# A bias add moved to GpSimd, a scale folded into a mask, and one rounding pass on VectorE

## The reference

```python
fake_quant(x): scale = absmax(x, axis) / bound;  q = round(clip(x / scale));  return q * scale
xq = fake_quant(conv, bits=8, axis=-1)      # one scale a row (sample, channel)
kq = fake_quant(kernel, bits=8, axis=0)     # one scale an output column
y  = xq @ kq + fake_quant(bias, bits=16)
out = x + fake_quant(y, bits=8, axis=-1)    # one scale a row
```

## Time and profile before

| what | value |
|---|---|
| median of 3 runs | 280.97 us (279.19 to 281.17) |
| the profiled execution | 278.56 us |
| its span | 276.7 us |
| TensorE busy | 251.1 us, 91% |
| VectorE busy | 238.8 us, 86% |
| ScalarE busy | 185.2 us, 67% |
| GpSimd busy | 153.8 us, 56% |

### The profile page before, as it was taken

The page is one execution under the profiler, slowest core; times in us unless marked ns, Lnnn a source line. Parts: engine busy times, 40 slices in busy tenths (PEclk is TensorE's granted clock), DMA queues, the critical chain, the costliest instruction groups (busy, mean ns, idle before and its releaser), DMA issues.

```text
span 276.7 us, 4240 instructions
## 1 busy us (share of the span) xinstructions
PE 251.1 (91%) x1372; PEld 163.5 (59%) x1372; DVE 238.8 (86%) x509; ACT 185.2 (67%) x278; POOL 153.8 (56%) x71
## 2 busy tenths in 40 slices
PE   7866769999999999999999999999999999997540
PEld 3555557666666666666666666666666666663210
DVE  1799964799999999999999999999999989999984
ACT  6257586477777777777777777777777767564762
POOL 2533333356666666666666666666666666533453
PEclk9979999999999999999999999999999999999996
DMA  6997322406666565566666766666666663333355
GB/s 253 416 408 301 123 84 103 153 0 227 223 203 212 211 202 212 203 217 217 209 204 210 230 228 228 228 227 226 219 203 197 218 218 117 144 142 139 107 220 219
DMA packets 15799, 56.04 MB, mean 203 GB/s; under 512 B 1954, under 2 KB 1954, under 8 KB 15778
## 3 DMA queue, kind: packets, MB, share of 16 engines
q1 hardware_dynamic: 15488, 55.71, 56.8%
q10 hardware_dynamic: 290, 0.07, 0.1%
HBM read 38.99 MB, written 16.78 MB: 202 GB/s over the span
## 4 chain that ended last, share of the span: by engine, by line
PE 81%; DVE 8%; ACT 4%; DMA 3%; issue 2%; SPq 0%; DVEq 0%
PE dense_ps L427 36%; PE conv_ps L396 31%; PE turn_ps L416 5%; PE conv_ps L386 5%; DMA k_raw<-ffn_kernel 3%; DVE dense_ps L550 2%; DVE y L559 2%; DVE y_max L604 2%; ACT kq L279 2%; PE small_ps L407 2%; PE dense_ps L449 1%; DVE k_max L523 1%; ACT a_int L304 1%; PE dense_ps L440 1%; ACT x_hi L265 1%
## 5 line engine op out<-in xcount | busy, mean ns | idle before, releaser
L427 PE MATMUL dense_ps<-kq,a_t 128*128 128x512 bf16 x512 | 120.6, 379 | 6.1 <-DVE y L559 5.0
L218 POOL TENSOR_TENSOR x_lo<-xwin,x_hi 128x1032 fp32r<-128x1032 f32 x32 | 76.6, 2393 | 80.8 <-ACT x_hi L265 80.8
L227 POOL TENSOR_TENSOR o_sb<-y,o_sb 128x1024 f32<-128x1024 f32 x31 | 73.9, 2384 | 32.8 <-ACT y L315 32.7
L427 PEld LDWEIGHTS dense_ps<-kq,a_t 128*128 128x128 bf16 x512 | 48.9, 101 | 53.7 <-issue 6.7
L295 ACT CAST a_t<-turn_ps 128x1024 bf16<-128x1024 int16 x32 | 32.4, 1012 | 48.5 <-PE turn_ps L416 48.5
L564 DVE TENSOR_REDUCE small_ps<-conv_ps 128x8 f32<-128x1024 f32 x32 | 39.4, 1232 | 13.8 <-PE conv_ps L396 13.5
L550 DVE SCALAR_TENSOR_TENSOR dense_ps<-dense_ps,row_scale,k_scale_b 128x512 f32<-128x512 f32 x64 | 47.7, 745 | 3.6 <-PE dense_ps L427 3.6
L312 ACT ACTIVATE y_int<-y,y_inv 128x1024 int16<-128x1024 f32 x31 | 35.6, 1148 | 22.3 <-DVE y_inv L611 22.1
L559 DVE TENSOR_TENSOR y<-dense_ps,bq 128x512 f32<-128x512 f32 x64 | 43.9, 685 | 2.8 <-ACT bq L288 1.6
L604 DVE TENSOR_REDUCE y_max<-y 128x1 f32<-128x1024 f32 x32 | 38.7, 1210 | 0.7 <-issue 0.2
L304 ACT ACTIVATE a_int<-conv_ps,inv 128x128 int16<-128x128 f32 x128 | 36.0, 363 | 1.1 <-DVE inv L590 1.1
(11 more groups left out here) (55 smaller groups left out, 160.2 us busy)
## 6 DMA issues: line engine op xcount, KB each, us to landing
xwin<-x_windows SPq DMA_DIRECT2D x32, 516.0 KB, 4.8
o_sb<-x_rows SPq DMA_DIRECT2D x32, 512.0 KB, 5.3
out<-o_sb SPq DMA_DIRECT2D x31, 512.0 KB, 2.9
k_raw<-ffn_kernel SPq DMA_DIRECT2D x4, 1024.0 KB, 10.5
w_raw<-taps SPq DMA_DIRECT2D x2, 256.0 KB, 3.2
b_row<-ffn_bias SPq DMA_DIRECT2D x1, 512.0 KB, 15.9
out<-o_sb SPq DMA_DIRECT2D x2, 256.0 KB, 2.7
condt<-cond_t ACTq DMA_DIRECT2D x1, 32.0 KB
```

The source lines that it names most:

```text
L218: pool.tensor_tensor(x_lo[:, at].rearrange("p n b -> p (n b)"), xwin[:, t % XWIN, :], x_hi[:, at].bitcast(F32).rearrange("p n b -> p (n b) ...
L227: pool.tensor_tensor(o_sb[:, at, :], y[:, t % YRING, :], o_sb[:, at, :], ALU.add).then_inc(s["o_made"], 1)
L427: mm = pe.matmul(dense_ps[:, h, :], a_t[:, t % LEVELS, q].rearrange("b j o -> b (j o)"), kq[:, q, half(h)], start=(q == 0), stop=(q == Q - 1))
```

## The change

The bias of the second half is added by GpSimd, in SBUF, in place. VectorE's scaling of that half now writes `y` in SBUF, since GpSimd's add reads it there. For the last tile both stay on VectorE, as before. GpSimd's new `add_bias(t, 1)` is the first step of its iteration t + 5, in front of `split` and `add_x`. `TAIL` becomes 6, so `out_scale`, `quantise`, `add_x` and the store of each tile come one iteration later. TensorE's `dense(t, 1)` waits for the scaling of the tile before, no longer for its bias. The factor 1/127 and the lower limit of the scale move from their own instruction (L582, removed) to the mask and the masking instruction, which becomes a `scalar_tensor_tensor`. VectorE rounds the levels of all eight samples in one instruction of 128x1024, and ScalarE's `round_levels` is gone.

```diff
-TAIL = LAG[1] + 1
+TAIL = LAG[1] + 2
...
+        def pool_adds(t, h):
+            return h == 1 and t < LAST
...
+            def add_bias(t, h):
+                wait(pool, f"scaled{h}", t + 1)
+                wait(pool, "b_made", 1)
+                pool.tensor_tensor(y[:, t % YRING, half(h)], y[:, t % YRING, half(h)],
+                                   bq[:, half(h)], ALU.add).then_inc(s[f"biased{h}"], 1)
...
             for k in range(TILES + TAIL):
+                if there(k - LAG[1] - 1) and pool_adds(k - LAG[1] - 1, 1):
+                    add_bias(k - LAG[1] - 1, 1)
                 if there(k + 2):
                     split(k + 2)
...
-            def round_levels(t):
-                ...
-                for n in range(NS // 2, NS):
-                    ins = act.activation(a_int[:, at, n * BLOCKS:(n + 1) * BLOCKS],
-                                         conv_cols(at)[:, n, :], ACT.Copy,
-                                         scale=inv8[:, at, n:n + 1])
...
             def dense(t, h):
                 wait(pe, "a_made", t + 1)
-                wait(pe, f"biased{h}", t)
+                wait(pe, "scaled1" if h else "biased0", t)
...
+            dve.wait_ge(s["mask_made"], 1)
+            dve.tensor_scalar(mask_q[:], mask[:], 1.0 / 127, None, ALU.mult
+                              ).then_inc(s["mask_q_made"], 1)
...
             def scale_half(t, h):
                 wait(dve, f"dense_made{h}", t + 1)
-                dve.scalar_tensor_tensor(out=dense_ps[:, h, :], in0=dense_ps[:, h, :],
+                if pool_adds(t, h):
+                    wait(dve, "o_made", t - YRING + 1)
+                    to = y[:, t % YRING, half(h)]
+                else:
+                    to = dense_ps[:, h, :]
+                dve.scalar_tensor_tensor(out=to, in0=dense_ps[:, h, :],
...
-                dve.tensor_tensor(col_max[:, t % 2], cmax_ps..., mask[:]..., ALU.mult)
+                dve.scalar_tensor_tensor(out=col_max[:, t % 2], in0=cmax_ps...,
+                                         scalar=127 * TINY, in1=mask_q[:]...,
+                                         op0=ALU.max, op1=ALU.mult)
...
-                dve.tensor_scalar(scale8[:, at], rmax_ps, 1.0 / 127, TINY, ALU.mult,
-                                  ALU.max).then_inc(s["scale_made"], 1)
+                dve.reciprocal(inv8[:, at], rmax_ps).then_inc(s["inv_made"], 1)
...
-                half_n = NS // 2
-                dve.tensor_tensor(a_int[:, at, 0:HALF]..., conv_cols(at)[:, 0:half_n, :], ...)
+                dve.tensor_tensor(a_int[:, at, :]..., conv_cols(at), ...)
...
                     scale_half(k - LAG[1], 1)
-                    add_bias(k - LAG[1], 1)
+                    if not pool_adds(k - LAG[1], 1):
+                        add_bias(k - LAG[1], 1)
```

More of the change, by code:

```diff
@@ L54, in build @@
         mask = sb("mask", [P, NS], F32)
+        mask_q = sb("mask_q", [P, NS], F32)
         same = sb("same", [P, CG], F32)
@@ L356, in _ @@
                     quantise(k - TAIL)
-                if there(k):
-                    round_levels(k)
             quantise_last()
@@ L380, in conv @@
                 x_at = t % XSPLIT
-                wait(pe, "a_rounded_dve", t - 1)
                 wait(pe, "a_rounded", t - 1)
@@ L559, in add_bias @@
                 dve.tensor_tensor(y[:, t % YRING, half(h)], dense_ps[:, h, :], bq[:, half(h)],
-                                  ALU.add).then_inc(s[f"biased{h}"], 1)
+                                  ALU.add).then_inc(s["biased_last" if h else "biased0"], 1)
             def column_max(t):
@@ L570, in column_max @@
                 if t == 0:
[L571 to L574, removed]
+                    dve.wait_ge(s["mask_q_made"], 1)
+                dve.scalar_tensor_tensor(out=col_max[:, t % 2],
+                                         in0=cmax_ps.unsqueeze(2).to_broadcast([P, NS, Q]),
+                                         scalar=127 * TINY,
+                                         in1=mask_q[:].unsqueeze(1).to_broadcast([P, NS, Q]),
+                                         op0=ALU.max, op1=ALU.mult
+                                         ).then_inc(s["col_max_masked"], 1)
             def levels(t):
@@ L581, in levels @@
                 wait(dve, "row_max_made", t + 1)
-                dve.tensor_scalar(scale8[:, at], rmax_ps, 1.0 / 127, TINY, ALU.mult,
-                                  ALU.max).then_inc(s["scale_made"], 1)
+                dve.reciprocal(inv8[:, at], rmax_ps).then_inc(s["inv_made"], 1)
                 wait(dve, "scaled1", t - RSRING + 1)
                 dve.tensor_tensor_reduce(out=picked[:, at], in0=rmax_ps, in1=mask[:],
-                                         scale=1.0 / 127, scalar=0.0, op0=ALU.mult, op1=ALU.add,
+                                         scale=1.0, scalar=0.0, op0=ALU.mult, op1=ALU.add,
                                          accum_out=row_scale[:, r_at:r_at + 1]
                                          ).then_inc(s["picked_made"], 1)
-                wait(dve, "scale_made", t + 1)
-                dve.reciprocal(inv8[:, at], scale8[:, at]).then_inc(s["inv_made"], 1)
                 wait(dve, "inv_made", t + 1)
                 wait(dve, "a_turned", t - 1)
-                half_n = NS // 2
-                dve.tensor_tensor(a_int[:, at, 0:HALF].rearrange("p (n b) -> p n b", b=BLOCKS),
-                                  conv_cols(at)[:, 0:half_n, :],
-                                  inv8[:, at, 0:half_n].unsqueeze(2)
-                                  .to_broadcast([P, half_n, BLOCKS]), ALU.mult
-                                  ).then_inc(s["a_rounded_dve"], 1)
+                dve.tensor_tensor(a_int[:, at, :].rearrange("p (n b) -> p n b", b=BLOCKS),
+                                  conv_cols(at),
+                                  inv8[:, at].unsqueeze(2).to_broadcast([P, NS, BLOCKS]),
+                                  ALU.mult).then_inc(s["a_rounded"], 1)
             def out_scale(t):
@@ L602, in out_scale @@
                 wait(dve, "biased0", t + 1)
-                wait(dve, "biased1", t + 1)
+                if pool_adds(t, 1):
+                    wait(dve, "biased1", t + 1)
+                else:
+                    wait(dve, "biased_last", 1)
                 dve.tensor_reduce(y_max[:, at], y[:, t % YRING, :], AX_X, ALU.max,
```

12 lines of the change are left out of this document (3 added, 9 removed).

## The result

The changed kernel takes 283.12 us (median of 4 runs, 282.83 to 283.36), the kernel before 280.08 us beside it: ratio 1.0107, 95% interval 1.0057 to 1.0157. That is 3.0 us more, against a forecast of 2.65, and 283.1 against 283.6. The kernel before takes near 279.1 or near 281.3 us from run to run, and two of its four runs here are of either kind (279.14 and 279.19, 280.97 and 281.17). The profiled execution of the changed kernel took 283.36 us with a span of 281.6. For it the forecast was 281.2, and against the profiled execution of before it is 4.8 us more.

What follows compares the result with a forecast made beforehand. TensorE was taken to bound the middle at 7.34 us an iteration, so only start and tail could change: -2.65 + 5.3 = +2.65 us, added to 280.97 for 283.6 us; range 280.8 to 286.8 us.

Steps and rivals of the forecast that it cites:

- The middle: nothing: Middle iterations: VectorE's 0.28 us saving is hidden by TensorE and GpSimd's added work fits; the period stays 7.34 us.
- The start, -2.65: Start: without ScalarE's roundings, the second tile's dense product starts at 38.8 instead of 41.4, so the middle begins 2.65 us earlier.
- the turn: Start: TensorE's turn of tile 0's levels, forecast near 24.3 instead of 25.99, 1.65 to 1.75 us earlier.
- The tail, +5.3: Tail: the extra iteration of lag is paid through GpSimd's queue and a last meeting with VectorE, ending 5.3 us later.
- if the maximum never waits for GpSimd: Tail: the sign that refutes the forecast, which had VectorE's maximum of `y` waiting for GpSimd's bias add.
- the loop: Tail: GpSimd's bias add behind `add_x(t-2)`, `quantise(t-2)` and `out_scale(t-2)`; one turn takes 7.76 us for two tiles.
- Rival 1: Start: GpSimd's subtraction gets in before the last weight rounding, VectorE loses 2.3 us, gain left 0.2: 286.1 us; 27%.
- the tie: Start: VectorE's last weight rounding and GpSimd's subtraction, forecast within 0.2 us of each other, VectorE first.
- Rival 2: Tail: not slower, only GpSimd's own work counts, +3.0 us; with the start's gain +0.35, 281.3 us; 18%.
- The sum: Whole kernel: -2.65 + 5.3 = +2.65 us, giving 281.2 us for the profiled execution and 283.6 us for the median.

Runs made afterwards that it cites:

- after_six: The changed kernel with six buffers of `y` instead of five: 282.18 us against 281.09 for the kernel before, ratio 1.0062.
- hybrid: The change without GpSimd's bias add, `TAIL` 5, only the first three tiles rounded in one VectorE pass: 277.04 us against 279.64 before, ratio 0.9904.
- after_warm: The changed kernel with 10 and 3 extra unread TensorE products in the gaps before its last two dense products: 282.55 us, ratio 1.0065 to the kernel before.
- lag_six: The kernel before with only `TAIL` 6 instead of 5 and six buffers of `y`: 284.42 us against 281.09, ratio 1.0142.
- bias_ahead: The changed kernel with `TAIL` 5 and GpSimd's bias add one iteration earlier, between `split` and `add_x`: 278.93 us against 279.64 before, ratio 0.9968.
- after_six_dve: The changed kernel with six buffers of `y` and VectorE adding the second bias from tile 26 on: 280.64 us against 279.64 before, ratio 1.0042.
- no_pool_bias: The changed kernel with both biases on VectorE and `TAIL` 5, mask and wide rounding kept: 278.17 us against 279.64 before, ratio 0.9933.
- delay_one: The changed kernel with one small VectorE instruction before the last pair of weight blocks: 286.71 us against 279.87 before, ratio 1.024.
- delay_four: The changed kernel with four small VectorE instructions before the last pair of weight blocks: 287.96 us against 279.87 before, ratio 1.0294.
- before_warm: The kernel before with 6 extra unread TensorE products in each gap before its last two dense products: 281.87 us against 281.36, ratio 1.0046.

## Why the prediction was right

- *The middle: nothing.* Right: 7.33 to 7.36 us an iteration in the changed kernel and in all its variants that I looked at, with VectorE from 6.4 to 7.1 us busy.
- *The start, -2.65.* Right: -2.83 in the profile by the arrival of the weights, and -2.7 in that of after_six. The runs of the hybrid, which has little else, give -2.7 by the ratio and -2.1 against the shorter runs of before. Both steps came near their places, less the late start of 0.69: the turn at 24.03 (forecast 24.3), the dense product at 38.59 (38.8).
- *The tail, +5.3.* The size is right at full clock (5.3 in after_six, 5.4 in after_warm), and too small by 1.5 for the changed kernel. The times came as forecast up to the maximum of tile 28, that one in part by luck: VectorE reached it over the held buffer and not over GpSimd's bias add. I had written that I was wrong "if the maximum never waits for GpSimd", and in the profile of the changed kernel it never does. What failed is the step that the hold on the five buffers is one "which the loop hides". At full clock it does, from tile 30 on (after_warm); but the wait left TensorE idle for 2.61 us, its clock fell, and its products, 2.8 us longer, overtook the loop by 1.5. TensorE's clock was not in the sum.
- *What I called the cause* needs correction. My chain runs through GpSimd's bias add, and the 7.76 us of its loop are confirmed (7.73 in after_six). But of the 6.8 us of the tail the loop adds only 1.5. The extra iteration of lag by itself costs 3.4 (lag_six), what is left of the change 0.4 (the wider rounding of tile 31 was forecast at 0.34), the held buffer with the clock 1.5. The GpSimd part had to pay for the lag because its bias stood behind the addition in the queue. bias_ahead, which needs no lag, is not slower than the kernel before.
- *Rival 1* did happen, in single executions (in the profiled ones of after_warm and after_six_dve). In the profile of the changed kernel VectorE won the tie by 0.06 us (35.49 against 35.55). A run of the hybrid (279.56 us) and one of no_pool_bias (280.48) stand out from the others in the same way, at a high mean clock, but no profile shows them. *Rival 2* (the tail at +3.0) did not happen, since the steps on ScalarE and VectorE are dependencies; GpSimd stands idle for them in the tail (2.89 us before its last addition).
- *The sum was met by luck.* For the profiled execution I forecast 281.2 us, and it took 283.36: 1.5 more in the tail, 0.7 by the late weights, 0.2 in the middle, less 0.2 in the start. The forecast of 283.6 for the median met 283.1 because I had added 2.4 us, by which the runs shown lay above the profile. That was the distance between the two groups of the kernel before, and the changed kernel's four runs (282.83 to 283.36) do not have it. And the 3.0 us measured are against a median of 280.08 over runs of both groups; against its two shorter runs there they are 4.0.

## What to carry to other kernels

An engine's relief pays only where that engine is in the chain: here taking ScalarE's four small roundings away was worth 2 to 2.7 us in the first three tiles and nothing in the other 29, so the change was worth making for three tiles. A later lag of one stage is free in the middle of a pipeline and is paid in full when it drains, in ring buffers held longer too; ask of each queue what stands behind what in the last iterations. A wait that looks hidden can cost through TensorE's clock: after idle times between 1.6 and 3.3 us the next products sometimes took up to 1.9 times as long here. And where the runs of a kernel fall into groups, compare with the runs of one group, or stage by stage between profiles; the ratio of mixed medians made a cost of 1.5 us look like 0.6.

## What was not expected of the hardware

- VectorE's back-to-back roundings of 128x1024 from SBUF to SBUF let GpSimd in between: 3.54 to 3.59 us for two instead of 1.42, whenever GpSimd's instruction had come while the first ran (after_warm, after_six_dve, delay_one, delay_four), and 2.93 us instead of 2.38 for GpSimd when it came during the second.
- TensorE's clock after a gap, for eight products that take 1.89 us at full clock. In the tail it stayed behind gaps of 1.67 us (before, lag_six) and up to 2.05 us (bias_ahead). Behind 2.2 to 2.3 us in the start it did either: 1.89 in the kernel before and in after_warm, 2.46 in after_six_dve, 3.37 in before_warm, 3.57 in delay_one and delay_four. In the tail it fell within the product behind a gap of 2.61 us (3.03) and 3.33 us (2.31), and the next one took 3.57; in delay_four it was back for the next one (3.13, then 1.89), where it had also fallen behind 2.28 us a tile earlier (16 products in 5.18 us instead of 3.61). It is no matter of the gap alone: with the same gap of 1.63 us and the same work in front of it, the second convolution's first product group of four took 1.91 us in the kernel before and 1.11 in after_warm.
- A last meeting of VectorE and GpSimd, both with two SBUF inputs, made an addition that takes 739 ns by itself last 2254 ns.
